# Turning a group's probabilities ahead of the slot's other TensorE work, in a hybrid two-layer kernel on one core

## The reference

```python
I = jnp.einsum('bths,h->bts', relu(q_i @ k_i), idx_w)      # the index: a score for each earlier token
_, idx = jax.lax.top_k(I, 96)                               # 64 newest tokens (forced) and the 32 best others
key_c, value = (c_kv @ W_uk)[idx], (c_kv @ W_uv)[idx]       # rows of the chosen tokens
scores = (q_c @ key_c + q_r @ key_r) * scale                # 8 heads
attn = jax.nn.softmax(scores, axis=-1)
out = (attn @ value) @ W_out
x = x + out
x = x + int_ffn(layernorm(x))                               # silu(x @ gate) * (x @ up) @ down
```

## Time and profile before

| | |
|---|---|
| median of three runs | 1310.84 us (1309.04 to 1316.33) |
| the profiled execution: its own time | 1308.47 us |
| its span, first to last instruction | 1306.6 us |
| around the span | 1.9 us |
| mean granted TensorE clock | 0.798 |
| busy: TensorE, VectorE, ScalarE, GpSimd | 1026.5, 788.5, 705.3, 577.7 us |

### The profile page before, as it was taken

How to read it: one execution, slowest core, us unless ns; L and a number is a source line. 1 busy time by engine, 2 the same in 40 slices (tenths; PEclk the granted TensorE clock), 3 DMA queues, 4 the chain that set the end, 5 groups by cost and what they waited for, 6 DMA issues and landing times. The chain is left out here.

```text
span 1306.6 us, 19767 instructions
## 1 busy us (share of the span) xinstructions
PE 1026.5 (79%) x6850; PEld 741.0 (57%) x6850; DVE 788.5 (60%) x1468; ACT 705.3 (54%) x1928; POOL 577.7 (44%) x614
## 2 busy tenths in 40 slices
PE   8999999999865978777887778766867681646887
PEld 6888676675523655554565555645645561435644
DVE  5898765756555776676577565565665480702346
ACT  5776554646354656556655565454654470515545
POOL 0210342533573655566556566565565617072001
PEclk9999999999975676678666678777787685856889
DMA  7000000000172243242132221221212212030000
GB/s 225 2 18 2 11 27 1 1 1 1 31 167 57 66 104 69 62 107 57 36 87 50 57 60 31 56 60 28 55 35 55 60 31 42 6 94 13 1 1 32
DMA packets 58737, 62.07 MB, mean 48 GB/s; under 512 B 27760, under 2 KB 43152, under 8 KB 58256
## 3 DMA queue, kind: packets, MB, share of 16 engines
q1 hardware_dynamic: 42768, 36.41, 10.7%
q0 software_dynamic: 15872, 24.41, 9.1%
HBM read 52.65 MB, written 8.13 MB: 47 GB/s over the span
## 5 line engine op out<-in xcount | busy, mean ns | idle before, releaser
L791 POOL DMA_INDIRECT gathered_rows<-key_table,idx_T x496 | 483.1, 974 | 367.2 <-issue 129.8
L2409 DVE TENSOR_TENSOR turned_rows<-bank,rank_rope 96x512 f32<-96x512 f32 x128 | 87.5, 684 | 224.2 <-remote 134.2
L1891 ACT ACTIVATE attn_out<-bank 32x128 f32<-32x128 f32 x128 | 33.6, 262 | 237.3 <-PE bank L835 113.5
L2383 DVE SCALAR_TENSOR_TENSOR index_sums<-index_relu,iw,index_sums 128x512 f32<-128x512 f32 (+4 forms) x114 | 76.0, 666 | 98.9 <-ACT index_relu L1845 61.8
L835 PE MATMUL bank<-keys_and_latents,q_window 96*128 96x80 f32 x256 | 59.6, 323 | 89.5 <-DVE x L2426 49.5
L1300 PE MATMUL bank<-ident,gathered_rows 128*96 128x128 f32 x512 | 101.9, 335 | 28.4 <-DVE turned_rows L2409 25.2
L835 PE MATMUL bank<-probs_window,local_values 80*32 80x128 f32 x256 | 63.6, 339 | 70.5 <-issue 41.8
L835 PE MATMUL bank<-index_k_hi,index_q 128*128 128x512 f32 (+5 forms) x160 | 88.5, 555 | 28.7 <-issue 14.9
L835 PEld LDWEIGHTS bank<-keys_and_latents,q_window 96*128 96x128 f32 x256 | 50.4, 245 | 103.1 <-DVE turned_rows L2409 52.7
L1845 ACT ACTIVATE index_relu<-bank 128x512 f32<-128x512 f32 (+4 forms) x152 | 76.2, 510 | 60.2 <-remote 28.0
L1300 PEld LDWEIGHTS bank<-ident,gathered_rows 128*96 128x96 f32 x512 | 72.0, 156 | 39.6 <-issue 36.3
(11 more groups left out here) (300 smaller groups left out, 2497.7 us busy)
## 6 DMA issues: line engine op xcount, KB each, us to landing
queries_in<-q_rot SPq DMA_DIRECT2D x32, 256.0 KB
gathered_rows<-key_table,idx_T POOLq DMA_INDIRECT x496
q_rot<-rotated SPq DMA_DIRECT2D x16, 256.0 KB
queries_in<-q_lat SPq DMA_DIRECT2D x16, 256.0 KB
h<-in_h SPq DMA_DIRECT2D x2, 1024.0 KB, 7.5
q_lat<-q_latent_sb SPq DMA_DIRECT2D x8, 256.0 KB
local_values<-key_table SPq DMA_DIRECT2D x15, 80.0 KB
rope_tables<-in_cos_ql SPq DMA_DIRECT2D x4, 256.0 KB
```

What stands on the lines that cost most here:

```text
L791: pool.indirect_dma_start(out=G[i % 2][:, gather_place(i, q), :], out_offset=None, in_=key_table[0:index_width(i), :], in_offset=bass.Indi ...
L1891: fn(dst, score_bank(n)[0:DC, 2 * P:3 * P].rearrange("c (q h t) -> c q h t", h=NH, t=QD), ACT.Copy)\
L2383: v.scalar_tensor_tensor(s_, r_, iw[:, h:h + 1], s_, ALU.mult, ALU.add).then_inc(i_used, 1)
L2409: v.tensor_tensor(GT[n % 2].rearrange("r (j p) -> r j p", j=4), bank[2][0:ROW, :].rearrange("r (j p) -> r j p", j=4), rank_rope[:].unsquee ...
```

## The change

`probs_turn(n-1)` moves from behind the slot's other TensorE work to a place right behind `values(n-2)`. Nothing is added or removed, and no other engine's stream changes: the orders of VectorE, ScalarE, GpSimd and SyncE are the same before and after.

```diff
                     if 0 <= n - 2 < GROUPS:
                         values(n - 2)
+                    if 0 <= n - 1 < GROUPS:
+                        probs_turn(n - 1)
                     for i, what, k in SLOT_STEPS[s]:
                         if what == "sum":
                             index_scores(i, k)
...
                         piece(c, k)
                     for c, k in tail_at(s):
                         tail_step(c, k)
-                    if 0 <= n - 1 < GROUPS:
-                        probs_turn(n - 1)
                     if 0 <= n - 2 < GROUPS and (n - 2) % NG == NG - 1:
                         out_project((n - 2) // NG)
```

## The result

The changed kernel takes 1327.27 us (median of 11 runs, 1319.86 to 1331.43), the kernel before 1310.84 us on the same chip (11 runs, 1301.18 to 1316.75). The ratio is 1.0126 with a 95% interval of 1.01 to 1.0151: 16.4 us slower, where 1324 us had been forecast. The profiled execution has a span of 1320.6 us, 14.0 us longer than before, and sits near the bottom of its runs.

A forecast was written before the change was run, and what follows sets the result against it. No engine is full; waits between engines bound the kernel. 12.3 us (slots without gathers) plus 2.7 (with) made 15.0 us on the profiled 1308.47: 1323.5, said as 1324 us, forecast range 1316 to 1334, eight times in ten 1308 to 1343.

The forecast's parts named there:

- the two sequences: TensorE waits for ScalarE ahead of the other work; ScalarE reads that work before the turned probabilities. All costs come from these.
- the faster rival: L1882's waits end earlier everywhere and free the copies: 1295 us with all 25.8 us back; chance 0.10.
- its sign of 50 us or more: In the changed trace, L1324's idle time ending with ACT L1876 should grow from 26.9 us to 50 us or more.
- The late slots: Slots without gathers, from 101 on: terms together 12.3 us slower, allowed 8 to 16.
- units: Slots 105, 109, 125: unit ready later, ScalarE idles 1.45 us, net 1.2 us each, 3.6 us.
- unit behind regrouping: Slot 106: two regrouping copies of ScalarE stand in front of the unit, leaving 0.8 us of loss.
- index units: Slots 101 to 104: two matmuls ready 0.4 us late for ScalarE in each, 1.6 us.
- norms, linear queries: Slots 113, 114, 120, 121, 126, 128, 129: larger matmuls that ScalarE reads come late, 0.7 us each, 4.9 us.
- down projections: Slots 111, 127: ScalarE reads nothing, but the projection delays TensorE's next rows by 0.7 us each, 1.4 us.
- taken as nothing: Steps that only fill a wait (kv, KV) and slots 108, 123, 124 around an output projection: no cost.
- the clock falls: Rival: a tenth less granted TensorE clock in the three late stretches, about 9 us more, 1333 us; chance 0.08.
- The gather slots: Slots 3 to 100: 2.7 us from twelve slots ending with an output projection; TensorE's late results cover all others.

The follow-up runs named there:

- the half change: New order only in slots 101 and up, old order elsewhere, against the kernel before: 1320.34 us beside 1311.53, ratio 1.0068.
- the other half: New order only in slots below 101, old order from slot 101 on, against the kernel before: 1316.2 us, ratio 1.0041.
- The pair without gathers: Kernel before and changed kernel, both without gathers of tiles 2 to 15 and the waits for them: 1092.64 and 1150.86 us, beside 1312.45 for the kernel before.
- one item ahead: Kernel before, with the transposes moved behind the first item of the slot's other work, ahead of the rest: 1306.39 us beside 1312.45, ratio 0.9966.

## Why the prediction was right

**The bound and the sign: right.** ScalarE reads the other work ahead of the turned probabilities, so transposes ahead of that work gain nothing and make the work late. L1882's waits fell from 38.2 to 3.9 us and nothing came of it. Of the two sequences that the forecast named, the first carries the loss: TensorE's stop now stands ahead of the other work. ScalarE's reading order is not needed for it, as the late stretches took 105.7 us with that order changed along and 106.3 without. Which wait ends last in each of these slots is not shown. The falling waits were the faster rival's whole case; it needed about half of them on the path (12.3 of 25.8 us is a little less than half, not more, as its text has it). One reading of the forecast was wrong without harm: the 26.9 us and 47 times of the earlier trace rows count stops twice, and it set its sign of 50 us or more by that total.

**The size: right in sum, with errors both ways in its terms.** The sum was 15.0 us on the profiled execution; that one grew by 14.0 us and the medians by 16.4. The late slots had 12.3 us of it. By the medians of the half change they cost 8.8 us, and by the traces of eight kernels 12 us; both lie in the 8 to 16 that the forecast allowed. Slots 118 to 130 grew by 9.0 us in the changed kernel and 6.3 us in the half change, where 6 had been forecast. By slot, from the start of one slot's values to the next in the two profiled executions:

| term | slots | predicted, us | measured, us |
|---|---|---|---|
| units | 105, 109, 125 | 3.6 | 2.3 |
| unit behind regrouping | 106 | 0.8 | 0.9 |
| index units | 101 to 104 | 1.6 | 1.5 |
| norms, linear queries | seven | 4.9 | 5.3 |
| down projections | 111, 127 | 1.4 | -0.3 |
| taken as nothing | 108, 123, 124 | 0 | 1.2 |
| norm of slot 130 | 130 | not in the sum | 1.6 |
| kv step | 119 | 0 | 1.8 |

That the terms meet their sums is in part luck. In four slots the clock was low in this execution (113, 119, 126 and 130, at 0.80, 0.60, 0.74 and 0.64), and they hold 8.2 of the 13.9 us. Slots 113 and 126 make 4.8 of the 5.3 us of the norms; in the half change slot 126 took 3.99 us at full clock instead of 5.60, so the term would have come out near 3.7.

*Units.* ScalarE waited 1.24 us where 1.45 had been worked out, and a slot grew by 0.7 to 0.9 us instead of 1.2. The 1.45 us had the durations one behind the other (0.33 + 1.13 us); after, L1324 starts at 1224.79 and the unit's last matmuls end at 1226.09, 1.30 us, since the matmuls overlap.

*Down projections.* This term failed. Slot 127 grew by 0.35 us instead of 0.7, and slot 111 became 0.6 us shorter. ScalarE reads nothing there, so its copy came earlier (L1882 waits 0.26 us in slot 127, where it waited 1.05), and I had let only TensorE's lateness count.

*A slot forgotten.* Slot 130 holds the last norm's variance. I had counted norms up to slot 129; L1947 waits 1.48 us for it.

*The clock.* The forecast's text calls itself wrong if the late clock falls below 0.85, and in the third stretch it is 0.83. So by its own sign this part fails: TensorE was busy for 4.4 us more, of the 9 us that the case "the clock falls" had priced. Only a part of this can be put down to the order. Slot 119 holds a kv step of 16 small matmuls that wait for nothing. The window over this slot, after and then before:

```profile
1197.80:1203.50 5.70, 5.70 (x50) 5.45 (x42) 0.71 (x4) 2.99 (x11) 0.00 (x0) 0.60 0.00 0
```

```profile
1194.90:1198.80 3.90, 3.90 (x46) 3.71 (x42) 0.68 (x3) 2.06 (x8) 0.00 (x0) 0.91 0.00 0
```

TensorE is busy for all of it both times; at a granted clock of 0.60 the same step takes 1.8 us more. But this does not come with the order. The same slot with the new order in the half change (late slots only), then with the old order in the other half:

```profile
1203.46:1207.18 3.72, 3.72 (x48) 3.56 (x42) 0.71 (x4) 2.98 (x11) 0.00 (x0) 0.96 0.00 0
```

```profile
1190.20:1194.80 4.60, 4.60 (x46) 4.38 (x42) 0.69 (x4) 2.08 (x8) 0.00 (x0) 0.76 0.00 0
```

In every trace with the gathers the clock is at 0.50, its lower level, through slot 118, behind the long stop near 1170 us; how far into slot 119 that lasts differs from one execution to the next. Slots 113 and 130 are another matter. Slot 130 is at 0.64, 0.50, 0.70 and 0.82 in the four traces with the new order there, and at 0.96 to 1.00 in the six with the old one. Slot 113 is at 0.80, 0.76 and 0.78 with the new order, or at 1.00 where ScalarE's order was changed along, and at 1.00 in all six with the old one. So in these two slots a lower clock goes with the new order. The section of the Trainium skill that the prediction weighed, "A second HAM failure mode: psum-queue depth-cycling" in "TensorE: Matmul & The Clock Gate", agrees in direction with slots 113 and 130; slot 119 and the first stretch, which rose to 1.00, do not bear it out. Whether the stops caused the fall was not tried apart from the order itself.

**The gather slots: right that they are covered, a little short in size.** 2.7 us were forecast and 4.7 measured, with an interval of about 2 to 9 us. The pair without gathers settles the assumption behind it, which was the forecast's weakest: the cover is real, and it goes when the gathers and the waits for their rows go. If it had failed altogether, the early slots would have lost 43 us, where the forecast had 39. The forecast's check that the tiles between 450 and 1040 us keep their pace holds within what one execution can show: the stretch from slot 8 to slot 101 took 606.1 us before and 600.8 after, while the medians say that it should have grown. A single trace doesn't price a change of 5 us there.

**Where the gain of one item ahead arises is open.** It can't be in slots 105 to 130, whose order is the old one. In its trace slots 8 to 100 take 9 us less than before, but the half change below slot 101, whose median is slower, shows 10 us less there as well, in an execution that lay 11 us under its median.

## What to carry to other kernels

Don't put a wait for another engine ahead of work that waits for nothing: what was free while it filled the wait becomes late for whoever reads it. Before moving work forward on one engine, read in which order the next engine reads, and what is then late ahead of it; but to let the reader take the early result early did not win the loss back here. Idle time before an instruction is no price: 39 us of new stops cost 16 us, 19 us of new stops under the gathers cost nothing, and with the index unit ahead of the values a wait fell by 20 us while the kernel lost 23. What a new order costs depends on what else holds up the slot: the early slots lost 4.7 us with the gathers and 43 us without. One piece of independent work in front of the wait was enough; whether a second costs or gains, the runs don't show.

## What the runs showed of the hardware

TensorE's results come late while GpSimd gathers, and it is a large effect. Beyond slot 50, the kernel before has two long stops; in this one the rows' transposes (L1300) are over by the record at 1084.4, and VectorE gets them 30 us later:

```profile
1083.35 1.09 PE L1300 MATMUL bank<-ident,gathered_rows 128*96 128x128 f32 x4
1114.77 0.69 DVE L2409 TENSOR_TENSOR turned_rows<-bank,rank_rope 96x512 f32<-96x512 f32 x1 [33.67 <-remote]
...
1115.80 0.69 PE L835 MATMUL bank<-keys_and_latents,q_window 96*128 96x80 f32 x2 [31.36 <-DVE x L2426]
```

Up to 1111.4 GpSimd issues gathers, one in 1.25 us (0.95 us each and 0.3 us between). Without the gathers of tiles 2 to 15, and without the waits for their rows, the slots with the long stops shrink (slot 107 from 43.6 to 12.5 us, slots 116 and 117 together from 38.9 to 7.6), slots 8 to 100 take 453 us instead of 606, the kernel takes 1092.64 instead of 1312.45 us, as expected before the run, and the mean clock rises from 0.798 to 0.882. So the gathers and the waits for them cost 220 us, beside which the 16 us of this change are small. The run took both away at once, so it doesn't say how much of the 220 us is waiting for data and how much is TensorE being held up; what holds it up is not shown.
